# One of eight one-hot products moved from VectorE to ScalarE in 34 scaled copies, base counts moved behind the first group of matmuls, and two moment products joined in one

## The reference

```python
ef = concatenate([x[src], x[dst], edge_attr])        # one row per edge
h = ef @ W1 + b1
mu, var = mean(h, axis=0), mean((h - mu) ** 2, axis=0)
h = relu((h - mu) * rsqrt(var + eps) * gamma + beta)
out = segment_sum(h @ W2 + b2, src) / (counts + 1) + x
x = layernorm(x + out)
# then three graph convolutions (x + conv(conv(conv(x)))) with the
# symmetric normalized adjacency over dst, and a layernorm
```

## Time and profile before

| what | value |
|---|---|
| median of 3 runs | 3799.39 us (3799.33 to 3801.58) |
| the profiled execution | 3800.09 us, span 3798.3 us |
| busy TensorE, VectorE, ScalarE, GpSimd | 3624.6, 2510.9, 1500.2, 962.0 us |
| phase one's loop | from about 93 to 1230 us of the span |
| moments and batch norm | from about 1234 to 1274 us |
| phase two's blocks | to about 2530 us |
| mean granted TensorE clock | 0.987 of full |

### The profile page before, as it was taken

One profiled execution on the slowest core, in us unless ns is written; L12 is line 12 of the kernel. 1 busy time (PEld: TensorE's weight loads), 2 busy tenths in 40 slices (PEclk: granted clock), 3 DMA queues, 4 the chain that ended last, 5 costly groups with the idle time before them and its releaser, 6 DMA issues.

```text
span 3798.3 us, 104239 instructions
## 1 busy us (share of the span) xinstructions
PE 3624.6 (95%) x40722; PEld 2585.7 (68%) x40943; DVE 2510.9 (66%) x3683; ACT 1500.2 (39%) x3822; POOL 962.0 (25%) x916
## 2 busy tenths in 40 slices
PE   4699999999998899999999999999999999999999
PEld 4588888888888677777777777774444544454444
DVE  6999999999995798898889888973111111111112
ACT  5355555455554466666666666662000000000000
POOL 3000000000000566676767667710000000000000
PEclk8899999999999899999999999999999999999999
DMA  7122322332234455555555555535666566656664
GB/s 246 53 88 87 101 87 85 97 91 87 85 103 148 136 156 157 157 155 156 158 156 154 159 157 156 153 134 182 197 195 200 187 199 196 200 183 211 205 208 133
DMA packets 428707, 569.35 MB, mean 150 GB/s; under 512 B 193778, under 2 KB 353452, under 8 KB 421708
## 3 DMA queue, kind: packets, MB, share of 16 engines
q1 hardware_dynamic: 396908, 510.29, 43.2%
q0 software_dynamic: 25088, 51.43, 5.0%
q10 hardware_dynamic: 6624, 6.42, 0.5%
HBM read 458.48 MB, written 109.53 MB: 150 GB/s over the span
## 4 chain that ended last, share of the span: by engine, by line
PE 92%; DVE 4%; ACT 1%; issue 1%; SPq 1%; DMA 1%; POOL 0%; ACTq 0%; DVEq 0%; POOLq 0%
PE py L1674 31%; PE ph L1364 11%; PE pY L861 11%; PE pSum L1383 10%; PE pbk L922 8%; PE ph L1367 7%; PE pA L848 3%; PE ph L1359 3%; PE pX L853 2%; PE pS L852 1%; PE pbk L899 1%; PE pbk L898 1%; ACT x L1030 1%; DVE prod_raw L1152 1%; PE pg L1660 1%
## 5 line engine op out<-in xcount | busy, mean ns | idle before, releaser
L1312 POOL DMA_INDIRECT q<-pq_dram,chosen x784 | 846.6, 1080 | 385.4 <-issue 198.5
L1674 PE MATMUL py<-ring_raw,p 128*128 128x512 bf16 (+1 forms) x3822 | 785.5, 368 | 4.7 <-DVE g L1792 2.8
L1364 PE MATMUL ph<-p,prod_raw 128*128 (+1 forms) x7056 | 683.2, 219 | 18.6 <-DVE prod_raw L1480 11.9
L1674 PEld LDWEIGHTS py<-ring_raw,p 128*128 128x128 bf16 x3822 | 362.6, 98 | 419.2 <-issue 4.4
L1364 PEld LDWEIGHTS ph<-p,prod_raw 128*128 128x128 bf16 x7056 | 492.6, 98 | 117.3 <-issue 0.7
L1428 ACT ACTIVATE x<-ph 128x512 bf16<-128x512 f32 x588 | 351.4, 598 | 454.2 <-PE ph L1367 320.7
L1367 PE MATMUL ph<-q,prod_raw 128*128 128x128 bf16 x4704 | 519.4, 219 | 0.0
L861 PE MATMUL pY<-p,ring_raw 128*128 128x128 bf16 x7203 | 501.7, 219 | 0.8 <-POOL ring_raw L793 0.4
L1383 PE MATMUL pSum<-x,ring_raw 128*128 128x384 bf16 x2401 | 498.8, 327 | 0.3 <-DVE x L1537 0.3
L1532 DVE SCALAR_TENSOR_TENSOR ring_raw<-ph,x 128x512 f32<-128x512 f32 x588 | 404.2, 687 | 121.2 <-ACT x L1428 121.2
L1850 DVE TENSOR_TENSOR yt<-py,dinv_row 128x512 f32<-128x512 f32 (+1 forms) x39 | 25.8, 661 | 684.1 <-PE py L1674 684.1
(11 more groups left out here) (338 smaller groups left out, 4407.9 us busy)
## 6 DMA issues: line engine op xcount, KB each, us to landing
ring_raw<-at_dram SPq DMA_DIRECT2D x252, 896.0 KB, 4.8
at_dram<-ring_raw SPq DMA_DIRECT2D x49, 1568.0 KB, 5.6
prod_raw<-lrow_dram SPq DMA_DIRECT2D x147, 384.0 KB
prod_raw<-lrow_dram SPq DMA_DIRECT2D x196, 256.0 KB
prod_raw<-lrow_dram SPq DMA_DIRECT2D x49, 416.0 KB
q<-pq_dram,chosen POOLq DMA_INDIRECT x784
arow_dram<-x SPq DMA_DIRECT2D x294, 36.8 KB
x<-arow_dram SPq DMA_DIRECT2D x147, 54.0 KB
```

The source lines that it names most:

```text
L1312: nc.gpsimd.indirect_dma_start(q_rows[i][:, k, :], None, pq_rows, bass.IndirectOffsetOnAxis(ap=chosen[u][:, i, k:k + 1], axis=0)).then_inc ...
L1364: last = nc.tensor.matmul(bank[:, k * P:(k + 1) * P], T[q][:, 0, at:at + P], p_b[:, :, m3, :].rearrange("p a d -> p (a d)"), start=False, ...
L1674: last = nc.tensor.matmul(py[par][:, 0:w], g3[c % 2][:, 7 * i + m, k, :], ring[i][:, 0:w // P, m, :], start=at == m == k == 0, stop=at == ...
```

## The change

Three parts.

1. In the loop the eighth product (field 7) of a block is no longer made by VectorE. ScalarE makes it: it first copies the last field of the record to 34 fp32 columns `rd`, and then, for each of the 34 columns i, copies the 49 one-hot values of that column from `hot_p` to `prod` with the column of `rd` as scale (`last_field`). Three of these follow each of the group copies 1 to 11, one follows group copy 12. `prod_ready` now counts twice a block: VectorE after field 6, ScalarE after its last copy. TensorE waits for both, SyncE too, and VectorE waits for it before it writes the next `hot_p`.
2. On TensorE the base counts and the transposes of a step stand behind group 0 instead of ahead of it (`bases`), and ScalarE's copies of both stand behind its copy of group 0.
3. In phase two one fp32 matmul for each node block takes the place of two: p is the stationary operand (128 columns), and the moving operand is p scaled by the node's count, with the three columns of `mom` beside it (131 columns). ScalarE makes the scaled p in seven copies a batch with a column as scale, and one copy of 21 `mom` values. The square sum is then the diagonal of the product (`own`, taken with `ident_f`, summed by a matmul with ones), and the sums of p are three columns, which one more matmul turns to rows.

```diff
 # VectorE
+                            if not (isinstance(s, int) and s == 0):
+                                dve.wait_ge(S["prod_ready"], s * 2)
                             V.tensor_tensor(hot_p, iota_blk[:].unsqueeze(1).to_broadcast(dims), pairs.to_broadcast(dims), ALU.is_equal).then_inc(S["hot_ready"], 1)
...
-                            for f in range(4, 8):
+                            for f in range(4, 7):
                                 last = product(f)
                             last.then_inc(S["prod_ready"], 1)
 # SyncE
-                            put(sp, S["prod_ready"], s)
+                            put(sp, S["prod_ready"], s * 2)
 # TensorE
+                    def both(s, m, par, half, bkt, h_, a_, y_):
...
                                 y_group(s, par, g)
+                            if g == 0:
+                                bases(s, m, par, bkt, h_)
...
-                            pe.wait_ge(S["prod_ready"], s + 1)
+                            pe.wait_ge(S["prod_ready"], s * 2 + 2)
 # ScalarE
+                    def last_field(s, par, lo, hi):
+                        if lo == 0:
+                            act.wait_ge(S["hot_ready"], s + 1)
+                            act.wait_ge(S["known_ready"], s + 1)
+                        for i in range(lo, hi):
+                            made = nc.scalar.activation(prod[:, i // 2, 7, :, i % 2], hot_p[:, i // 2, :, i % 2], ACT.Copy, scale=rd[:, i:i + 1])
+                        if hi == TPB:
+                            made.then_inc(S["prod_ready"], 1)
...
                             nc.scalar.activation(abuf[u][:, 4 * g:4 * g + w, :], ...).then_inc(S["a_ready"], 1)
+                            if g == 0:
+                                bases(s, m, par, bkt, h_)
+                            elif bkt:
+                                last_field(s, par, 3 * g - 3, min(3 * g, TPB))
...
                             act.wait_ge(S["key_ready"], s + 1)
+                            nc.scalar.activation(rd[:, 0:TPB], rec[par][:, 9, :], ACT.Copy)
...
-                            evacuate(s, m, par)
+                            evacuate(s, m, par, bkt, h_)
+                        else:
+                            bases(s, m, par, bkt, h_)
+                            if bkt:
+                                last_field(s, par, 0, TPB)
 # phase two, TensorE
-                            nc.tensor.matmul(pSum[0][0:3, 0:D], mom[:, 7 * i + j, :], pf[:, 7 * i + j, :], start=i == j == 0, stop=i == j == 6)
-                            last = nc.tensor.matmul(pSum[1][0:3, 0:D], mom[:, 7 * i + j, :], psq[i % 2][:, j, :], start=i == j == 0, stop=i == j == 6)
+                            last = nc.tensor.matmul(pSum[0][:, 0:D + 3], pf[:, 7 * i + j, :], psq[i % 2][:, j, :], start=i == j == 0, stop=i == j == 6)
...
                     pe.wait_ge(S["weighed"], 2)
+                    nc.tensor.matmul(pSum[1][0:3, 0:D], p_sums, ident_f[:], start=True, stop=True).then_inc(S["p_turned"], 1)
+                    pe.wait_ge(S["weighed"], 3)
+                    nc.tensor.matmul(st[:, D:2 * D], ones_f[:], own, start=False, stop=False)
+                    pe.wait_ge(S["weighed"], 4)
                     nc.tensor.matmul(st[:, 0:D], ones_f[0:3, :], xs[0:3, 2 * D:3 * D], start=False, stop=False)
-                    nc.tensor.matmul(st[:, D:2 * D], ones_f[0:3, :], xs[0:3, 0:D], start=False, stop=False)
-                    nc.tensor.matmul(st[:, D:2 * D], ones_f[0:3, :], xs[0:3, D:2 * D], start=False, stop=True).then_inc(S["stats_made"], 1)
+                    nc.tensor.matmul(st[:, D:2 * D], ones_f[0:3, :], xs[0:3, 0:D], start=False, stop=True).then_inc(S["stats_made"], 1)
 # phase two, ScalarE
+                    act.wait_ge(S["moments_in"], 1)
...
-                        nc.scalar.activation(psq[i % 2][:], pf[:, 7 * i:7 * i + 7, :], ACT.Square).then_inc(S["squared"], 1)
+                        for j in range(7):
+                            nc.scalar.activation(psq[i % 2][:, j, 0:D], pf[:, 7 * i + j, :], ACT.Copy, scale=mom[:, 7 * i + j, 0:1])
+                        nc.scalar.activation(psq[i % 2][:, :, D:D + 3], mom[:, 7 * i:7 * i + 7, :], ACT.Copy).then_inc(S["squared"], 1)
 # phase two, VectorE
-                    for u in range(2):
-                        link(V.tensor_tensor(xs[0:3, u * D:(u + 1) * D], cf[0:3, u * D:(u + 1) * D], pSum[u][0:3, 0:D], ALU.mult))
-                    link(V.tensor_tensor(xs[0:3, 2 * D:3 * D], cf[0:3, D:2 * D], pSum[0][0:3, 0:D], ALU.mult))
+                    V.tensor_copy(p_sums, pSum[0][:, D:D + 3]).then_inc(S["weighed"], 1)
+                    V.tensor_tensor(own, pSum[0][:, 0:D], ident_f[:], ALU.mult).then_inc(S["weighed"], 1)
+                    dve.wait_ge(S["p_turned"], 1)
+                    link(V.tensor_tensor(xs[0:3, 0:D], cf[0:3, 0:D], pSum[1][0:3, 0:D], ALU.mult))
+                    link(V.tensor_tensor(xs[0:3, 2 * D:3 * D], cf[0:3, D:2 * D], pSum[1][0:3, 0:D], ALU.mult))
```

More of the change, by code:

```diff
@@ L863, in y_group, with bases @@
                             last.then_inc(S["y_ready"], 1)
[L865 to L890, removed]
+                    def bases(s, m, par, bkt, h_):
                         if bkt:
@@ L908, in step, with moments @@
                             last.then_inc(S["turned"], 1)
+                    def both(s, m, par, half, bkt, h_, a_, y_):
+                        if a_:
+                            pe.wait_ge(S["hsd_ready"], (s - 2) * 2 + (half + 1))
+                            if half == 0 and not (isinstance(s, int) and s < 3):
+                                pe.wait_ge(S["t_read"], s - 2)
+                        groups = neighbours(s, par, half) if a_ else range(*HALVES[half])
+                        for g in groups:
+                            if y_:
+                                if g == 0:
+                                    pe.wait_ge(S["a_final"], s - 2)
+                                    if not (isinstance(s, int) and s < 4):
+                                        pe.wait_ge(S["y_kept"], s - 3)
+                                y_group(s, par, g)
+                            if g == 0:
+                                bases(s, m, par, bkt, h_)
+                    def moments(s, par, y_, st_):
+                        if st_:
+                            pe.wait_ge(S["y_kept"], s - 3)
+                            last = nc.tensor.matmul(pM[:, 0:2 * D + 7], qp[par], ym[par], start=False, stop=False)
+                        if isinstance(s, int) and s == B + 3:
+                            last = nc.tensor.matmul(pM[:], onesb[:], zerob[:, 0:2 * D].unsqueeze(1).to_broadcast([P, 2, 2 * D]), start=False, stop=True)
+                        if st_:
+                            last.then_inc(S["m_used"], 1)
+                    def step(s, m, par, bkt, h_, a_, y_, st_):
+                        moments(s, par, y_, st_)
                         if isinstance(s, int) and s == 1:
@@ L915, in step @@
                             nc.tensor.matmul(pY[:, 2 * D:4 * D], b2rep, mx[:], start=True, stop=True).then_inc(S["proj_ready"], 1)
-                        both(s, par, 0, a_, y_)
-                        both(s, par, 1, a_, y_)
+                        both(s, m, par, 0, bkt, h_, a_, y_)
+                        both(s, m, par, 1, bkt, h_, a_, y_)
                         if bkt:
-                            pe.wait_ge(S["prod_ready"], s + 1)
+                            pe.wait_ge(S["prod_ready"], s * 2 + 2)
                             pe.wait_ge(S["orank_ready"], s + 1)
@@ L1231, in build @@
                 mom = sb("mom", [P, B, 3]); xs = sb("xs", [4, 3 * D])
-                psq = [x1_free[:, u * 7 * D:(u + 1) * 7 * D].rearrange("p (j d) -> p j d", d=D) for u in range(2)]
+                psq = [x1_free[:, u * 7 * (D + 3):(u + 1) * 7 * (D + 3)].rearrange("p (j d) -> p j d", d=D + 3) for u in range(2)]
                 s_raw = sb("s_raw", [P, D]); dinv_rows = sb("dinv_rows", [P, D])
@@ L1235, in build @@
                 nb = [sb(f"nb{u}", [P, D], BF16) for u in range(3)]
+                own, p_sums = bt[0][:], bt[1][:, 0:3]
                 ph = [ps(f"ph{u}", [P, 512]) for u in range(4)]
```

21 lines of the change are left out of this document (12 added, 9 removed).

## The result

The changed kernel takes 3873.9 us (median of 4 runs, 3873.6 to 3875.4) against 3799.6 us before (4 runs): a ratio of 1.0195, 95% interval 1.0179 to 1.0210. That is 74 us slower. The forecast was 3863, with a range from 3828 to 3915.

The account below looks back on a forecast made before the run. TensorE, with VectorE nearly as tight, bounds the old loop; the change makes ScalarE the bound. 3800.1 + 64.4 (loop) - 5.4 (moments) = 3859.1 us, plus 4 for two clock falls, 3863.1; forecast 3863, range 3828 to 3915.

Parts of the forecast that it names:

- ScalarE becomes the bound; spacing 0.226, group 1.17: Loop groups: scaled copies start 0.226 us apart, so a group costs ScalarE 1.17 us against TensorE's 1.108.
- L922 at +17.52, idle 1.90, step +1.41: Loop step: the 34 rank matmuls start at +17.52 us, TensorE idles 1.90, each of 47 steps is 1.41 longer.
- VectorE's 0.96 buys little: Loop: one product less cuts VectorE from 21.94 to 20.98 us a step, only keeping it from becoming the bound.
- The clock allowance, two falls of 2 us: Loop: the 1.90 us gap may cost TensorE's clock in a few steps; two falls of 2 us add 4.
- the second rival: Loop: TensorE's clock falls in the new gap; one step in four gives +30 us, 3889; chance 0.13.
- my forecast's mechanism: Loop: ScalarE is the bound with a scaled-copy spacing of 0.21 to 0.24 us, giving 3840 to 3888; chance 0.68.
- The sign that I had set for it: Loop: a granted clock under 0.98 would show the forecast wrong and the clock rival true.
- Step 2 like the rest: Loop step 2: waited for VectorE, will wait for ScalarE; counted like the other steps, 1.41 us longer.
- Steps 0 and 1, -1.9: First two loop steps, which wait for VectorE's ranks: one product less saves 0.96 us each, 1.9 together.
- Moments, -5.4: Phase two's moment products: end 5.7 us earlier, 0.3 us more up to the first statistic, net -5.4 us.
- the third rival: Loop: scaled copies writing every second bf16 are slow, spacing 0.40 us, 272 us in 47 steps, 4131; chance 0.06.
- the first rival: Loop: scaled copies fit at spacing 0.131 us, ScalarE waits for TensorE, last copy decides; 3792 to 3796; chance 0.08.

Follow-up runs that it names:

- B alone: Against the kernel before: only base counts and transposes moved behind group 0, all eight products on VectorE; ratio 0.9980.
- B and C: Against the kernel before: base counts behind group 0 plus the one moment product, eighth product on VectorE; ratios 0.9968 and 0.9964.
- C alone: Against the kernel before: only the one moment product, loop as before; ratios 0.9979 and 0.9977.
- the split kernel: Against the change: only 18 of 34 columns as ScalarE scaled copies, the other 16 in one VectorE product; 3767.4 us.

## Why the prediction was right, point by point

- **ScalarE becomes the bound; spacing 0.226, group 1.17.** Right: 0.226 and 1.16. The constant scale, which changes nothing but the spacing, turns the loss into a gain.
- **L922 at +17.52, idle 1.90, step +1.41.** Right in kind, a little large: time zero is 713.05, the product starts at +17.38, the wait is 1.77, and a step without a clock fall is 1.24 us longer on average. The difference is mostly eleven groups of 1.155 and not 1.17, and that is the group copy: I put it at 0.49 from start to start, though the two starts that I gave for it lie 0.48 apart, and it measures 0.477. Behind group 12 I was 0.04 too low instead (0.15 and a last scaled copy of 0.41, for 0.20 and 0.32).
- **VectorE's 0.96 buys little.** Right as to the whole change. B alone shows what it is worth where ScalarE has room: without it VectorE takes back 0.3 us of a step.
- **The clock allowance, two falls of 2 us.** The mis-sized term: 13 falls of 1.6 us, 21 against 4. It was the second rival, forecast for one step in four with a chance of 0.13: it is 13 of 46, at 1.6 and not 2.5 us, so both my forecast's mechanism and this rival came true together. The sign that I had set for it, a granted clock under 0.98 in the loop, was a poor one: with all these falls the loop's mean still reads 0.98. I took the price from step 2, where the clock was already down as the product began; here it falls only at the product's start. How little may decide, the run with the last copy moved shows: with 0.16 us less of wait twelve of the falls are gone, on what may be another chip.
- **Step 2 like the rest.** Too small: it took 3.7 us more, not 1.4. It has no product with p, so TensorE's groups are short there, it waits 0.3 to 0.7 us for ScalarE ahead of most of them, and the whole of ScalarE's chain shows:

```profile
154.11 8.72 PE L926 MATMUL pbk<-prod_raw,q 128*128 128x392 bf16 x34 [1.91 <-ACT prod_raw L984]
```

- **Steps 0 and 1, -1.9.** They gave 1.8 (1.3 ahead of the first cells and 0.5 in the next step).
- **Moments, -5.4.** Measured -4.5 (1336.10 - 1314.58 against 26.02 before), and 1.3 more ahead of them, in the stretch that holds the steps without a block, where I had said that nothing is gained. I had 18 us from the first scaled copy to the end of the products; it is 18.6:

```profile
1314.58 2.15 ACT L1437 ACTIVATE x<-prod_raw,mom 128x128 f32<-128x128 f32 x7
```

```profile
1333.24 0.16 DVE L1527 COPY bt<-pSum 128x3 f32<-128x3 f32 x1 [5.67 <-PE pSum L1353]
...
1336.10 0.29 DVE L1535 TENSOR_TENSOR bt<-st,s_raw 128x128 f32<-128x128 f32 x1 [0.80 <-PE st L1364]
```

- **The first and the third rival.** The scaled copies don't fit: dead. Writes to every second element cost nothing that shows, with a spacing of 0.226 as for the scaled copies of rows 7 and not 0.40: dead. But the first rival's picture (ScalarE waits for TensorE, the last copy decides) is exactly what the constant scale shows: I had the product at the old place for it, and it starts 0.2 us earlier.

The sum, by its own terms: loop 64.4 and 4 of clock forecast, 79.9 measured (59 without the 13 falls); moments -5.4 forecast, -5.8 with what leads to them; everything behind, 0 forecast, 1.2 measured. That 3863 lies only 11 us off is in part luck: the loop without the clock was put 5 us too high and the clock 17 us too low.

## What to carry to other kernels

An engine that shows half its time idle has room only if the work can be placed where that idle time is: compare the period of the stage (1.108 us a group) with the sum of what the helper issues in it, instruction by instruction. When the sum comes out a few per cent above the period, move less: on top of B and C, 18 copies took 17 us off the loop's 46 steps, where 34 put 87 on them (1099.1 - 1012.4). And count what a wait of TensorE may cost beside its own length: waits of 1.69 to 1.79 us once in a step went with 13 falls of the clock, 21 us, and a wait 0.16 us shorter with one.

## What I had not expected

- A wait ahead of the product of 1.61 us brought the clock down in one of 46 steps, and one of 1.77 us in 13, in a stage where TensorE is otherwise busy throughout.
- With 56 more TensorE instructions in a step, TensorE waited up to 3.3 us once in each turn of the hardware loop, and the instruction queue had 240 packets against 59; it looks like a wait for instructions. As filling, three long instructions served here where 28 short ones did harm.
- On two chips what stands behind the loop is slower for every kernel that ran there. Between 1800 and 2400 us TensorE is busy 499.8 of 600 us in C alone there, and 600 of 600 in the split kernel on another chip; ScalarE waits 273 us for a releaser that the trace doesn't know. That it is the gathers landing late was not tested. The stretch in C alone (columns as above), and a wait between 1300 and 3300 us:

```profile
1800.00:2400.00 600.00, 499.83 (x5636) 375.00 (x5717) 424.16 (x662) 291.99 (x549) 312.67 (x313) 0.97 0.41 121
```

```profile
ACT x L1441 <- remote: 273.1, 96, 7.2
```
